# Sums of squares moved ahead of the score maximum, and a Newton step moved off GpSimd, in a six-layer windowed-attention stack

## The chip, the cores and the metric

One core of a Trainium2 chip. The metric is device time of one execution in microseconds (us); each time given for a kernel is the median of several runs. The program uses all engines of the core: TensorE (PE), VectorE (DVE), ScalarE (ACT), GpSimd (POOL) and SyncE (SP) as DMA queue.

## The reference, cut to what matters

The program is four residual blocks on x of shape 2 x 1024 x 128: a 16-head attention with a polynomial in place of softmax, a stack of six layers, a causal softmax attention, and the same stack of six layers again. The stacks are the long part and the only one that changes. One layer of a stack:

```python
def attn_layer(x, Wqkv, qs, ksc, Wo):            # 16 heads of 64, windows of 32
    q, k, v = split(x @ Wqkv)
    q = l2norm(q) * qs
    k = l2norm(k) * ksc
    q = q * cos * scale + rotate_half(q) * sin * scale
    k = k * cos * inv + rotate_half(k) * sin * inv
    return local_attention(q, k, v) @ Wo         # softmax over 64 keys

def ffn_layer(x, g, bln, W1, b1, W2, b2):
    mu = x.mean(-1, keepdims=True)
    var = ((x - mu) ** 2).mean(-1, keepdims=True)
    xn = (x - mu) / jnp.sqrt(var + 1e-05) * g + bln
    a, gate = jnp.split(xn @ W1 + b1, 2, -1)
    return a * gelu(gate) @ W2 + b2

for i in range(6):
    x = attn_layer(shift_tokens(x), ...) + x
    x = ffn_layer(shift_tokens(x), ...) + x
```

All arithmetic here is float32. An inverse root (of a sum of squares of q or k, or of the variance) is taken as a seed y = exp(-0.5 ln v) on ScalarE and one Newton step y(1.5 - 0.5 v y^2).

## The kernel before

`ffn_stack` works in slots. A slot s takes one tile of 128 tokens (16 tiles a layer, 6 layers, 96 tiles a stack, n is the tile's number) through the projections, and in the same slot other stages work on earlier tiles: the scores and the softmax on tile n-1, the transpose of the probabilities on n-2, the product with V on n-3, the output projection on n-4. The feed-forward net works on blocks of four tiles (512 tokens); `feed(s, lag)` gives the block whose turn it is, so that its steps fall into slots by s mod 4, the phase: phase 0 has the centred x, its square and the variance (lag 8) and the last hidden chunk (lag 12); phase 1 has the scaling by the inverse root (lag 9) and the output product (lag 13); phase 2 the three gate products (lag 10); phase 3 the gelu and two hidden chunks (lag 11).

The order on each engine is written out by hand, one function for each engine with a loop over the slots, and semaphores tie them. What each engine does in a slot, in its order:

- TensorE: project q into PSUM banks PQ; transpose the normalised q of n-1 into PT_S (waits `nrm`, 1) and the k (L1233, waits `nrm`, 2); project k into PK; mask and scores of n-1 into PT_S; project v; `values(n-3)`; the first two feed-forward products; then in `feed_third` a wait on `sbd`, by which VectorE says that it has read the scores out of PT_S; in phase 2 the third gate product; `out(s)`, the output projection (L1152, it writes the first bank of PT_S); in phases 0 and 1 a fourth feed-forward product; the transposes of O (L1276, wait `rot` and `sqd` of tile n). Then the next slot's q projection (L1097).
- ScalarE: copy O_T out (L1294); square q into `sq` (L1284, `sqd`); copy q_T, k_T; square k; in phase 3 the gelu; copy V; copy O; exp of the scores (L1332); Ln and Exp of the sums of squares (L1336, L1338, `seeded`); in phase 0 Ln and Exp of the variance (L1342, L1344); in phase 2 three gate copies.
- VectorE: three rope products of q (L1426 to L1429); the transpose of the probabilities (L1460, `ppt`); three rope products of k; row maximum (L1466) and shift (L1469, `sbd`); the two sums of squares (L1435) and their clamp (L1477, `clamped`); row sum (L1480) and its reciprocal (L1484, `rid`); feed-forward steps, among them the variance's epsilon (L1494) in phase 0 and in phase 1 the scaling (L1501) and two H or G writes (L1510); two adds of the output projection (L1515). At the end of a stack also the adds of two SBUF tensors at L1521.
- GpSimd: adds of the rope products of q and k (L1374); a Newton step of four small operations on 128x32 (L1376 to L1382); the products of q and k with the inverse norm (L1386, `nrm`); the product of E with the row's inverse (L1392, `pn`); in phase 0 a Newton step of four operations on 128x512 for the variance (L1396 to L1402, `f_nt`); in phase 1 the bias of xn (L1405).

Of the kernel before, what the change touches and what calls it, by code (L numbers as in the profile page):

```python
# [18 lines left out]
ALU = mybir.AluOpType  # L19
# [835 lines left out]
def ffn_stack(nc, ins, m, call):  # L855
# [6 lines left out]
    with ctx:  # L862
# [3 lines left out]
        def sig(name, per=1):  # L866
# [64 lines left out]
        f_xc, f_sq, f_xcs, f_var, f_eps, f_seed = sig("x_centered"), sig("x_squared"), sig("x_centered_copied"), \  # L931
            sig("var_done"), sig("eps_added"), sig("var_seeded", 2)
        f_nt, f_xn, f_xb = sig("var_newton_steps", 4), sig("xn_scaled"), sig("xn_ready")
        f_g, f_gev, f_ge, f_a, f_hm = sig("gate_done", 3), sig("gate_evacuated", 3), sig("gelu_done"), \
# [34 lines left out]
        def live(s):  # L969

            return 0 <= s < SLOTS
# [10 lines left out]
        def blk(b):  # L982

            return call * (SLOTS // TB) + b
# [295 lines left out]
        def _(act):  # L1280
# [8 lines left out]
            for s in slots:  # L1289
# [30 lines left out]
                if feed(s, 11) is not None:  # L1320
                    nc.scalar.preload_act_table_set("natural_log_exp_and_others")
                if live(s - 3):
                    act.wait_ge(o_mm.sem, o_mm.at(n - 3))
                    act.wait_ge(o_tr.sem, o_tr.past(n - 4))
                    nc.scalar.activation(O[:], PQ, ACT.Copy).then_inc(o_cp.sem, 1)
# [4 lines left out]
                if live(s - 1):  # L1330
                    act.wait_ge(sbd.sem, sbd.at(n - 1))
                    nc.scalar.activation(E[(n - 1) % 2][:], E[(n - 1) % 2][:], ACT.Exp).then_inc(expd.sem, 1)  # L1332
                if live(s):
                    act.wait_ge(clamped.sem, clamped.at(n))
                    act.wait_ge(newton.sem, newton.past(n - 1))
                    nc.scalar.activation(lg[:], ss[n % 2][:], ACT.Ln).then_inc(seeded.sem, 1)  # L1336
                    act.wait_ge(seeded.sem, seeded.at(n, 1))
                    nc.scalar.activation(y0[:], lg[:], ACT.Exp, scale=-0.5).then_inc(seeded.sem, 1)  # L1338
                if (b := feed(s, 8)) is not None:
                    act.wait_ge(f_eps.sem, f_eps.at(blk(b)))  # L1340
                    act.wait_ge(f_nt.sem, f_nt.past(blk(b) - 1))
                    nc.scalar.activation(xsq[:], var[:], ACT.Ln).then_inc(f_seed.sem, 1)  # L1342
                    act.wait_ge(f_seed.sem, f_seed.at(blk(b), 1))
                    nc.scalar.activation(vy0[:], xsq[:], ACT.Exp, scale=-0.5).then_inc(f_seed.sem, 1)  # L1344
                if (b := feed(s, 10)) is not None:
                    act.wait_ge(f_y.sem, f_y.past(blk(b) - 1))
                    for j, (o, k) in enumerate(FCH):
                        act.wait_ge(f_g.sem, f_g.at(blk(b), j + 1))
                        nc.scalar.activation(ge[0:k, j, :], bank((6, 7, 5)[j])[0:k], ACT.Identity,
                                             bias=b1[b // NBLK % 2][0:k, 3 + j:4 + j]).then_inc(f_gev.sem, 1)  # L1350

        @block.gpsimd
        def _(pool):
# [14 lines left out]
            for s in slots:  # L1368
# [20 lines left out]
                if live(s - 1):  # L1389
# [3 lines left out]
                                            ALU.mult).then_inc(pn.sem, 1)  # L1393
                if (b := feed(s, 8)) is not None:
                    pool.wait_ge(f_seed.sem, f_seed.at(blk(b)))
                    nc.gpsimd.tensor_tensor(xsq[:], vy0[:], vy0[:], ALU.mult).then_inc(f_nt.sem, 1)  # L1396
                    pool.wait_ge(f_nt.sem, f_nt.at(blk(b), 1))
                    nc.gpsimd.tensor_tensor(xsq[:], xsq[:], var[:], ALU.mult).then_inc(f_nt.sem, 1)
                    pool.wait_ge(f_nt.sem, f_nt.at(blk(b), 2))
                    nc.gpsimd.tensor_scalar(xsq[:], xsq[:], -0.5, 1.5, ALU.mult, ALU.add).then_inc(f_nt.sem, 1)  # L1400
                    pool.wait_ge(f_nt.sem, f_nt.at(blk(b), 3))
                    nc.gpsimd.tensor_tensor(var[:], xsq[:], vy0[:], ALU.mult).then_inc(f_nt.sem, 1)  # L1402
                if (b := feed(s, 9)) is not None:
# [7 lines left out]
        def _(dve):  # L1411
# [41 lines left out]
            for s in slots:  # L1453
                n = tile(s)
                if live(s):
                    rotate(s, 0, q_mm, PQ)
                if live(s - 2):
                    dve.wait_ge(pn.sem, pn.at(n - 2))
                    dve.wait_ge(pair_in[(n - 3) % 2].sem, pair_in[(n - 3) % 2].past((n - 3) // 2))
                    nc.vector.transpose(PT[:].rearrange("p b t -> p (b t)"), E[n % 2][:]).then_inc(ppt.sem, 1)  # L1460
                if live(s):
                    rotate(s, 1, k_mm, PK)
                if live(s - 1):
                    e = E[(n - 1) % 2]
# [7 lines left out]
                        .then_inc(sbd.sem, 1)  # L1472
                if live(s):
                    sums(n, 0)
                    sums(n, 1)
                    dve.wait_ge(red.sem, red.at(n))
                    nc.vector.tensor_scalar(ss[n % 2][:], ss[n % 2][:], 1e-24, None, ALU.max).then_inc(clamped.sem, 1)  # L1477
                if live(s - 1):
# [16 lines left out]
                if (b := feed(s, 9)) is not None:  # L1495
                    if b % NBLK == 0:
                        dve.wait_ge(ffn_in.sem, ffn_in.at(call * DEPTH + b // NBLK))
                    dve.wait_ge(f_nt.sem, f_nt.at(blk(b)))
                    dve.wait_ge(f_g.sem, f_g.past(blk(b) - 1))
# [97 lines left out]
```

## Time and profile before

| | |
|---|---|
| median of 3 runs | 4362.58 us (4357.62 to 4364.63) |
| the profiled execution | 4365.13 us |
| its span, first to last instruction | 4363.3 us |
| mean granted TensorE clock | 0.974 |
| PE, busy | 3866.2 us, 89% |
| DVE, busy | 3296.5 us, 76% |
| ACT, busy | 2534.1 us, 58% |
| POOL, busy | 2498.8 us, 57% |
| POOL waiting for the seed, L1376 <- L1338 | 476.6 us in 192 times |
| DVE waiting for the square of q, L1426 <- L1284 | 376.2 us in 188 times |

The two stacks lie at about 412 to 2142 us and 2625 to 4356 us of the span; the rest is the two attention blocks. A share of busy time is over the whole span; the shares say which engines have room, not which chain of waits sets a slot's length. For that one follows, within a slot, what each instruction waited for.

### The profile page before, as it was taken

The numbers are of one execution on the slowest core, as the hardware profiler recorded it, in microseconds if no ns is written. First come the engines' busy times: TensorE is split into PE (matmuls) and PEld (weight loads), VectorE is DVE, ScalarE is ACT, GpSimd is POOL, SyncE is SP. The second block draws the span as 40 slices with busy tenths as digits, with TensorE's granted clock in tenths as the row PEclk, the third lists the DMA queues.
The fourth block names the chain that finished last, engine by engine and source line by source line (L and its number), as shares of the span: only waits on it lengthen the run. The fifth ranks groups of instructions, "written<-read, shape, count | busy, mean of one in ns | idle before, by whom it ended". The sixth has DMA issues, their size and how long they took to land. (4 is left out here: it accounts for less than half of the span.)

```text
span 4363.3 us, 151598 instructions
## 1 busy us (share of the span) xinstructions
PE 3866.2 (89%) x66488; PEld 2314.4 (53%) x66488; DVE 3296.5 (76%) x4385; ACT 2534.1 (58%) x3236; POOL 2498.8 (57%) x2036
## 2 busy tenths in 40 slices
PE   6887799999999999999778877899999999999997
PEld 3323456665665666665433334566666666666664
DVE  7997777888888787888454436788888878878884
ACT  6885456566665666666324444556566565666654
POOL 0001677777777777777100005786777777777773
PEclk8999999999999999999789998999999999999998
DMA  0001232332323233222000002323323223232221
GB/s 19 1 1 42 72 87 65 85 77 75 83 67 87 73 78 85 62 67 62 17 1 1 1 14 74 92 62 84 81 67 85 73 79 80 73 81 71 66 60 40
DMA packets 165593, 260.83 MB, mean 60 GB/s; under 512 B 58572, under 2 KB 79816, under 8 KB 164936
## 3 DMA queue, kind: packets, MB, share of 16 engines
q1 hardware_dynamic: 164936, 251.13, 22.2%
q8 instruction: 528, 8.65, 0.9%
q14 instruction: 129, 1.06, 0.1%
HBM read 48.61 MB, written 1.05 MB: 11 GB/s over the span
## 5 line engine op out<-in xcount | busy, mean ns | idle before, releaser
L1374 POOL TENSOR_TENSOR f_k_rotated<-f_rope_ak,f_rope_bk 128x1024 f32<-128x1024 f32 x192 | 454.5, 2367 | 288.7 <-DVE f_rope_bk L1429 288.7
L1097 PE MATMUL banks<-f_wqkv,H 128*128 128x512 f32 x1152 | 564.9, 614 | 17.4 <-DVE f_E L1469 9.2
L1097 PE MATMUL banks<-f_wqkv,G 128*128 128x512 f32 x1152 | 551.8, 601 | 0.0
L1426 DVE TENSOR_TENSOR f_rope_aq<-banks,f_rope 128x1024 f32<-128x1024 f32 x192 | 235.1, 1225 | 389.5 <-ACT f_sqq L1284 376.2
L1361 POOL MEMSET f_kT<- 128x256 f32 x2 | 0.6, 311 | 839.9 <-POOLq L514 460.5
L1374 POOL TENSOR_TENSOR f_q_rotated<-f_rope_aq,f_rope_bq 128x1024 f32<-128x1024 f32 x192 | 454.5, 2367 | 29.0 <-DVE f_rope_bq L1429 28.6
L1319 ACT ACTIVATE f_V<-banks 128x1024 f32<-128x1024 f32 x192 | 196.8, 1025 | 418.7 <-PE banks L1097 418.3
L1152 PEld LDWEIGHTS banks<-f_O_T,f_wo 128*128 128x128 f32 x3072 | 372.6, 192 | 98.3 <-issue 94.6
L1152 PE MATMUL banks<-f_O_T,f_wo 128*128 128x128 f32 x3072 | 375.4, 275 | 6.4 <-issue 5.2
L1392 POOL TENSOR_TENSOR f_E<-f_E,f_row_inverse 128x1024 f32<-128x1024 f32 x192 | 368.6, 1920 | 19.8 <-DVE f_row_inverse L1484 19.8
L1386 POOL TENSOR_TENSOR f_q_rotated<-f_q_rotated,f_inverse_norm 128x1024 f32<-128x1024 f32 x192 | 365.2, 1902 | 15.0
L1386 POOL TENSOR_TENSOR f_k_rotated<-f_k_rotated,f_inverse_norm 128x1024 f32<-128x1024 f32 x192 | 366.2, 1907 | 0.0
L1129 PEld LDWEIGHTS banks<-f_V_previous,f_P_T_paired 64*32 64x32 f32 x12288 | 263.0, 105 | 163.9 <-issue 157.2
L1129 PE MATMUL banks<-f_V,f_P_T_paired 64*32 64x64 f32 x12288 | 323.4, 225 | 17.4 <-issue 16.3
L1426 DVE TENSOR_TENSOR f_rope_ak<-banks,f_rope 128x1024 f32<-128x1024 f32 x192 | 233.4, 1216 | 139.0 <-ACT f_sqk L1284 138.0
L1129 PE MATMUL banks<-f_V_previous,f_P_T_paired 64*32 64x64 f32 x12288 | 316.3, 225 | 12.5 <-issue 8.7
L1233 PE MATMUL banks<-ident,f_k_rotated 128*128 128x128 f32 x1536 | 213.4, 284 | 122.2 <-POOL f_k_rotated L1386 121.9
L1376 POOL TENSOR_TENSOR f_rsqrt_tmp<-f_rsqrt_seed 128x32 f32<-128x32 f32 x192 | 45.9, 239 | 476.6 <-ACT f_rsqrt_seed L1338 476.6
L1114 PEld LDWEIGHTS banks<-f_kT,f_qT 64*32 64x32 f32 x24576 | 271.0, 105 | 86.6 <-issue 62.7
L1114 PE MATMUL banks<-f_kT,f_qT 64*32 64x64 f32 x24576 | 305.1, 225 | 1.6 <-ACT f_kT L1307 1.5
L1138 PE MATMUL banks<-f_xn,f_w 128*128 128x512 f32 (+1 forms) x576 | 287.6, 623 | 19.1 <-DVE H L1510 12.0
L1460 DVE STREAM_TRANSPOSE f_P_T<-f_E 128x1024 f32<-128x1024 f32 x192 | 238.1, 1240 | 86.9 <-POOL f_E L1392 86.7
(207 smaller groups left out, 8961.6 us busy)
## 6 DMA issues: line engine op xcount, KB each, us to landing
f_P_T_paired<-f_P_T SPq DMA_DIRECT2D x1536, 64.0 KB
f_V_previous<-f_V SPq DMA_DIRECT2D x192, 384.0 KB, 3.7
f_V_previous<-f_V SPq DMA_DIRECT2D x192, 128.0 KB, 2.4
f_wqkv<-in_L_ffn_Wqkv SPq DMA_DIRECT2D x48, 384.0 KB, 4.1
f_rope<-in_rope SPq DMA_DIRECT2D x24, 512.0 KB, 5.1
f_wo<-in_L_ffn_Wo SPq DMA_DIRECT2D x12, 512.0 KB, 5.4
f_w<-in_L_ffn_W SPq DMA_DIRECT2D x12, 341.0 KB
f_w<-in_L_ffn_W SPq DMA_DIRECT2D x24, 64.0 KB
```

Source lines behind the costliest of these rows:

```text
L1097: mm = nc.tensor.matmul(ps[:, o * BLK:(o + 1) * BLK], xs, w[:, c * INNER + o * BLK:c * INNER + (o + 1) * BLK], start=True, stop=True)
L1114: mm = nc.tensor.matmul(PT_S[g * W:(g + 1) * W, c:c + 2 * W], qT[rows, k, g * W:(g + 1) * W], kT[u][rows, k, g * W:(g + 2) * W], start=Fal ...
L1129: mm = nc.tensor.matmul(PQ[g * W:(g + 1) * W, a * BLK + j * DH:a * BLK + (j + 1) * DH], F[n % 2][r, t, c * W:(c + 1) * W], of[n % len(of)] ...
L1138: nc.tensor.matmul(banks[0:k, bk * BLK:(bk + 1) * BLK], w1[b // NBLK % 2][:, half * DI + o:half * DI + o + k], xn[:], start=True, stop=Tru ...
L1152: mm = nc.tensor.matmul(bank(4, P), wo[layer(s - 4) % 2][:, k, :], OT[n % 2][:, :, m2, hh * 2 * W:(hh + 1) * 2 * W], start=k == 0, stop=k ...
L1233: mm = nc.tensor.transpose(PV_F[:, k * P:(k + 1) * P], qk[1][:, k * P:(k + 1) * P], ident[:])
L1319: nc.scalar.activation(V[n % 4][:], PV_F, ACT.Copy).then_inc(v_ev.sem, 1)
L1374: nc.gpsimd.tensor_tensor(qk[i][:], ra[i][:], rb[i][:], ALU.add).then_inc(radd.sem, 1)
L1386: nc.gpsimd.tensor_tensor(heads_of(qk[i][:]), heads_of(qk[i][:]), over(rn[:, i * HEADS:(i + 1) * HEADS], DH), ALU.mult)\
L1392: nc.gpsimd.tensor_tensor(e, e, ri[:].unsqueeze(1).unsqueeze(3).to_broadcast([P, 2, HEADS, W]), ALU.mult).then_inc(pn.sem, 1)
L1426: nc.vector.tensor_tensor(heads_of(ra[i][:]), src, table(2 * i, 0, DH), ALU.mult).then_inc(rot.sem, 1)
L1460: nc.vector.transpose(PT[:].rearrange("p b t -> p (b t)"), E[n % 2][:]).then_inc(ppt.sem, 1)
```

## The change

Three edits, all in `ffn_stack`.

1. VectorE's order: `sums(n, 0)` now stands right behind the rope products of q (ahead of L1460), and `sums(n, 1)` with the clamp right behind the rope products of k, ahead of the row maximum and the shift.
2. ScalarE's order: Ln and Exp of the sums of squares now stand behind the copy of V, ahead of the copy of O, the square of the centred x and the exp of the scores.
3. The variance's Newton step: GpSimd's four operations go. ScalarE squares the seed behind its Exp, in phase 0; VectorE does the rest in two operations in phase 1, ahead of the scaling.

```diff
@@ scalar
+                if live(s):
+                    act.wait_ge(clamped.sem, clamped.at(n))
+                    act.wait_ge(newton.sem, newton.past(n - 1))
+                    nc.scalar.activation(lg[:], ss[n % 2][:], ACT.Ln).then_inc(seeded.sem, 1)
+                    act.wait_ge(seeded.sem, seeded.at(n, 1))
+                    nc.scalar.activation(y0[:], lg[:], ACT.Exp, scale=-0.5).then_inc(seeded.sem, 1)
                 if live(s - 3):
                     act.wait_ge(o_mm.sem, o_mm.at(n - 3))
...
-                if live(s):
...
-                    nc.scalar.activation(y0[:], lg[:], ACT.Exp, scale=-0.5).then_inc(seeded.sem, 1)
...
                     nc.scalar.activation(vy0[:], xsq[:], ACT.Exp, scale=-0.5).then_inc(f_seed.sem, 1)
+                    act.wait_ge(f_seed.sem, f_seed.at(blk(b), 2))
+                    nc.scalar.activation(xsq[:], vy0[:], ACT.Square).then_inc(f_seed.sem, 1)
@@ gpsimd
-                if (b := feed(s, 8)) is not None:
-                    pool.wait_ge(f_seed.sem, f_seed.at(blk(b)))
-                    nc.gpsimd.tensor_tensor(xsq[:], vy0[:], vy0[:], ALU.mult).then_inc(f_nt.sem, 1)
...
-                    nc.gpsimd.tensor_tensor(var[:], xsq[:], vy0[:], ALU.mult).then_inc(f_nt.sem, 1)
@@ vector
                 if live(s):
                     rotate(s, 0, q_mm, PQ)
+                    sums(n, 0)
                 if live(s - 2):
...
                 if live(s):
                     rotate(s, 1, k_mm, PK)
+                    sums(n, 1)
+                    dve.wait_ge(red.sem, red.at(n))
+                    nc.vector.tensor_scalar(ss[n % 2][:], ss[n % 2][:], 1e-24, None, ALU.max).then_inc(clamped.sem, 1)
                 if live(s - 1):
...
-                if live(s):
-                    sums(n, 0)
-                    sums(n, 1)
...
                 if (b := feed(s, 9)) is not None:
...
+                    dve.wait_ge(f_seed.sem, f_seed.at(blk(b)))
+                    nc.vector.scalar_tensor_tensor(xsq[:], var[:], -0.5, xsq[:], ALU.mult, ALU.mult).then_inc(f_nt.sem, 1)
+                    dve.wait_ge(f_nt.sem, f_nt.at(blk(b), 1))
+                    nc.vector.scalar_tensor_tensor(var[:], xsq[:], 1.5, vy0[:], ALU.add, ALU.mult).then_inc(f_nt.sem, 1)
```

The sizes of the semaphores `f_seed` (2 to 3 steps) and `f_nt` (4 to 2) follow.

VectorE in the middle of a slot, before:

```order
L1426 TENSOR_TENSOR f_rope_aq<-banks,f_rope 128x1024
L1427 TENSOR_TENSOR f_rope_bq<-banks,f_rope 128x16x32
L1429 TENSOR_TENSOR f_rope_bq<-banks,f_rope 128x16x32
L1460 STREAM_TRANSPOSE f_P_T<-f_E 128x1024
L1426 TENSOR_TENSOR f_rope_ak<-banks,f_rope 128x1024
L1427 TENSOR_TENSOR f_rope_bk<-banks,f_rope 128x16x32
L1429 TENSOR_TENSOR f_rope_bk<-banks,f_rope 128x16x32
L1466 TENSOR_REDUCE f_row_max<-banks 128x16
L1469 TENSOR_TENSOR f_E<-banks,f_row_max 128x16x2x32
L1435 TENSOR_REDUCE f_sum_of_squares<-f_sqq 128x16
L1435 TENSOR_REDUCE f_sum_of_squares<-f_sqk 128x16
L1477 TENSOR_SCALAR f_sum_of_squares<-f_sum_of_squares 128x32
```

and now:

```order
L1419 TENSOR_TENSOR f_rope_aq<-banks,f_rope 128x1024
L1420 TENSOR_TENSOR f_rope_bq<-banks,f_rope 128x16x32
L1422 TENSOR_TENSOR f_rope_bq<-banks,f_rope 128x16x32
L1428 TENSOR_REDUCE f_sum_of_squares<-f_sqq 128x16
L1454 STREAM_TRANSPOSE f_P_T<-f_E 128x1024
L1419 TENSOR_TENSOR f_rope_ak<-banks,f_rope 128x1024
L1420 TENSOR_TENSOR f_rope_bk<-banks,f_rope 128x16x32
L1422 TENSOR_TENSOR f_rope_bk<-banks,f_rope 128x16x32
L1428 TENSOR_REDUCE f_sum_of_squares<-f_sqk 128x16
L1459 TENSOR_SCALAR f_sum_of_squares<-f_sum_of_squares 128x32
L1463 TENSOR_REDUCE f_row_max<-banks 128x16
L1466 TENSOR_TENSOR f_E<-banks,f_row_max 128x16x2x32
```

Both sums and the clamp have moved ahead of the row maximum and the shift (L1469 before, L1466 now).

VectorE at the end of a slot of phase 1, now:

```order
L1472 TENSOR_REDUCE f_row_sum<-f_E 128x16
L1476 RECIPROCAL f_row_inverse<-f_row_sum 128x16
L1491 SCALAR_TENSOR_TENSOR f_x_squared<-f_var_then_rstd,f_x_squared 128x512
L1493 SCALAR_TENSOR_TENSOR f_var_then_rstd<-f_x_squared,f_var_seed 128x512
L1497 SCALAR_TENSOR_TENSOR f_xn<-f_x_centered,f_ln_g_ln_b_b_1,f_var_then_rstd 128x512
L1506 SCALAR_TENSOR_TENSOR H<-banks,f_ln_g_ln_b_b_1,G 64x512 x2
L1511 TENSOR_TENSOR G<-banks,G 64x128 x2
```

The rows L1491 and L1493 are new there; both read two tensors in SBUF.

ScalarE at the end of a slot of phase 0, now:

```order
L1325 ACTIVATE f_log_sum<-f_sum_of_squares 128x32
L1327 ACTIVATE f_rsqrt_seed<-f_log_sum 128x32
L1331 ACTIVATE f_O<-banks 128x1024
L1335 ACTIVATE f_x_squared<-banks 128x512
L1338 ACTIVATE f_E<-f_E 128x1024
L1342 ACTIVATE f_x_squared<-f_var_then_rstd 128x512
L1344 ACTIVATE f_var_seed<-f_x_squared 128x512
L1346 ACTIVATE f_x_squared<-f_var_seed 128x512
L1294 ACTIVATE f_O_T<-banks 128x1024
L1284 ACTIVATE f_sqq<-banks 128x1024
```

L1346 is new, ahead of the O_T copy and the next slot's square of q; the two 128x32 rows stood behind the exp of f_E before.

## Rows read from the trace of the kernel before

**Rows 1.** Busy time by engine over most of the first stack: window, its length, each engine's busy us (instructions), granted PE clock, DMA share, GB/s.
```profile
620.00:2060.00 1440.00, 1353.54 (x26343) 873.93 (x26343) 1171.07 (x1505) 883.06 (x1107) 1078.56 (x876) 1.00 0.29 74
```

**Rows 2.** Who waited for whom, TensorE: total us, times, longest.
```profile
PE banks L1233 <- POOL f_k_rotated L1386: 121.9, 182, 1.2
```

**Rows 3.** Timeline of GpSimd, phase 2 and the next: start us, us, engine, line, operation.
```profile
1008.54 2.36 POOL L1374 TENSOR_TENSOR f_k_rotated<-f_rope_ak,f_rope_bk 128x1024 f32<-128x1024 f32 x1 [1.73 <-DVE f_rope_bk L1429]
...
1014.58 0.22 POOL L1380 TENSOR_SCALAR f_rsqrt_tmp<-f_rsqrt_tmp 128x32 f32<-128x32 f32 x1
...
1015.21 1.90 POOL L1386 TENSOR_TENSOR f_q_rotated<-f_q_rotated,f_inverse_norm 128x1024 f32<-128x1024 f32 x1
1017.07 1.90 POOL L1386 TENSOR_TENSOR f_k_rotated<-f_k_rotated,f_inverse_norm 128x1024 f32<-128x1024 f32 x1
...
1031.63 0.22 POOL L1380 TENSOR_SCALAR f_rsqrt_tmp<-f_rsqrt_tmp 128x32 f32<-128x32 f32 x1
```

**Rows 4.** Timeline of VectorE, one slot of phase 1.
```profile
1053.91 1.22 DVE L1426 TENSOR_TENSOR f_rope_aq<-banks,f_rope 128x1024 f32<-128x1024 f32 x1 [2.77 <-ACT f_sqq L1284]
...
1056.25 1.23 DVE L1460 STREAM_TRANSPOSE f_P_T<-f_E 128x1024 f32<-128x1024 f32 x1
1057.41 1.19 DVE L1426 TENSOR_TENSOR f_rope_ak<-banks,f_rope 128x1024 f32<-128x1024 f32 x1
...
1059.71 1.21 DVE L1466 TENSOR_REDUCE f_row_max<-banks 128x16 f32<-128x1024 f32 x1
1060.95 1.23 DVE L1469 TENSOR_TENSOR f_E<-banks,f_row_max 128x1024 f32<-128x1024 f32 x1
1062.09 1.21 DVE L1435 TENSOR_REDUCE f_sum_of_squares<-f_sqq 128x16 f32<-128x1024 f32 x1
1063.22 1.21 DVE L1435 TENSOR_REDUCE f_sum_of_squares<-f_sqk 128x16 f32<-128x1024 f32 x1
...
1064.56 1.21 DVE L1480 TENSOR_REDUCE f_row_sum<-f_E 128x16 f32<-128x1024 f32 x1
...
1065.97 0.69 DVE L1501 SCALAR_TENSOR_TENSOR f_xn<-f_x_centered,f_ln_g_ln_b_b,f_var_then_rstd 128x512 f32<-128x512 f32 x1
...
1068.32 0.61 DVE L1515 TENSOR_TENSOR H<-banks,H 64x128 f32<-64x128 f32 x2
```

**Rows 5.** Timeline of VectorE, a later slot of phase 1, 14 blocks on.
```profile
2032.16 0.69 DVE L1501 SCALAR_TENSOR_TENSOR f_xn<-f_x_centered,f_ln_g_ln_b_b,f_var_then_rstd 128x512 f32<-128x512 f32 x1
```

**Rows 6.** Timeline of TensorE, end of a slot of phase 2 and start of the next.
```profile
1013.42 1.95 PE L1152 MATMUL banks<-f_O_T,f_wo 128*128 128x128 f32 x16
1015.21 1.04 PE L1276 MATMUL banks<-ident,f_O 128*128 128x128 f32 x8
1016.08 1.88 PE L1097 MATMUL banks<-f_wqkv,H 128*128 128x512 f32 x4
```

**Rows 7.** Timeline of ScalarE, end of a slot of phase 0 and start of the next.
```profile
1050.66 0.63 ACT L1342 ACTIVATE f_x_squared<-f_var_then_rstd 128x512 f32<-128x512 f32 x1 [2.71 <-DVE f_var_then_rstd L1494]
...
1051.86 1.01 ACT L1294 ACTIVATE f_O_T<-banks 128x1024 f32<-128x1024 f32 x1
1052.76 1.02 ACT L1284 ACTIVATE f_sqq<-banks 128x1024 f32<-128x1024 f32 x1
```

**Rows 8.** Timeline of VectorE: the shift in that slot of phase 0.
```profile
1043.73 1.22 DVE L1469 TENSOR_TENSOR f_E<-banks,f_row_max 128x1024 f32<-128x1024 f32 x1
```

**Rows 9.** Timeline of VectorE: the adds at L1521 beside GpSimd's products, and alone.
```profile
2050.50 4.35 DVE L1521 TENSOR_TENSOR X<-X,H 64x512 f32<-64x512 f32 x2
...
2102.60 1.40 DVE L1521 TENSOR_TENSOR X<-X,H 64x512 f32<-64x512 f32 x2
```

**Rows 10.** Timeline of GpSimd: the k product that runs beside those adds.
```profile
2051.95 2.35 POOL L1386 TENSOR_TENSOR f_k_rotated<-f_k_rotated,f_inverse_norm 128x1024 f32<-128x1024 f32 x1
```

**Rows 11.** Timeline of TensorE: transposes after a long wait near the first stack's start.
```profile
464.94 1.97 PE L1227 MATMUL banks<-ident,f_q_rotated 128*128 128x128 f32 x8 [4.25 <-POOL f_q_rotated L1386]
```

**Rows 12.** Busy time and granted clock in the stretch that begins there, columns as in rows 1.
```profile
465.00:470.00 5.00, 5.00 (x18) 3.95 (x19) 1.34 (x2) 2.21 (x3) 5.00 (x3) 0.50 0.00 2
```

More of the change, by code:

```diff
@@ L931, in ffn_stack @@
         f_xc, f_sq, f_xcs, f_var, f_eps, f_seed = sig("x_centered"), sig("x_squared"), sig("x_centered_copied"), \
-            sig("var_done"), sig("eps_added"), sig("var_seeded", 2)
-        f_nt, f_xn, f_xb = sig("var_newton_steps", 4), sig("xn_scaled"), sig("xn_ready")
+            sig("var_done"), sig("eps_added"), sig("var_seeded", 3)
+        f_nt, f_xn, f_xb = sig("var_newton_steps", 2), sig("xn_scaled"), sig("xn_ready")
         f_g, f_gev, f_ge, f_a, f_hm = sig("gate_done", 3), sig("gate_evacuated", 3), sig("gelu_done"), \
@@ L1332, in _ @@
                     nc.scalar.activation(E[(n - 1) % 2][:], E[(n - 1) % 2][:], ACT.Exp).then_inc(expd.sem, 1)
-                if live(s):
[L1334 to L1337, printed above, removed]
-                    nc.scalar.activation(y0[:], lg[:], ACT.Exp, scale=-0.5).then_inc(seeded.sem, 1)
                 if (b := feed(s, 8)) is not None:
@@ L1393, in _ @@
                                             ALU.mult).then_inc(pn.sem, 1)
-                if (b := feed(s, 8)) is not None:
-                    pool.wait_ge(f_seed.sem, f_seed.at(blk(b)))
-                    nc.gpsimd.tensor_tensor(xsq[:], vy0[:], vy0[:], ALU.mult).then_inc(f_nt.sem, 1)
[L1397 to L1401, printed above, removed]
-                    nc.gpsimd.tensor_tensor(var[:], xsq[:], vy0[:], ALU.mult).then_inc(f_nt.sem, 1)
                 if (b := feed(s, 9)) is not None:
@@ L1472, in _ @@
                         .then_inc(sbd.sem, 1)
-                if live(s):
-                    sums(n, 0)
-                    sums(n, 1)
-                    dve.wait_ge(red.sem, red.at(n))
-                    nc.vector.tensor_scalar(ss[n % 2][:], ss[n % 2][:], 1e-24, None, ALU.max).then_inc(clamped.sem, 1)
                 if live(s - 1):
```

## The prediction

> **What bounds the kernel now.** I read the busy times first. Over most of the first stack TensorE is busy 1353.54 of 1440 us at full clock [rows 1], and no other engine comes near; a slot there lasts 17.25 us, so TensorE's own work is 17.25 x 0.94 = 16.2 and about 1 us a slot is waiting. The 17.25 comes from the scaling in phase 1, which recurs every four slots: (2032.16 - 1065.97) / 14 = 69.0 us a group [rows 4, 5]. The list of waits says whom TensorE waits for: the normalised k, 121.9 us in 182 times [rows 2]. GpSimd's timeline shows a period free of jitter, 1014.58 to 1031.63, 17.05 us [rows 3]. So I followed the chain of k backwards: k transposed and the next k projected on TensorE, squared, rope products, row maximum, shift, both sums and clamp on VectorE, Ln and Exp, then on GpSimd the Newton step and the products of q and k, and transposed again. That is a loop over one slot, and its sum is the 17.05. The change cuts this loop. The question is what the next loop is.
>
> **The change, part by part.** *The k loop.* The clamp of k now comes before the row maximum and the shift (59.71 to 62.09, 2.38 us) and without the sum of q behind them (1.13) [rows 4]: 3.5 us earlier. GpSimd must first finish its add of k, 2.36 us [rows 3], so 3.0 of it arrives and the loop falls to 14.05. It no longer binds.
>
> *The loop through the shift.* TensorE may not write the output projection before VectorE has read the scores (`sbd`). Write S for the end of the shift. From S the loop runs: output projection 1.79, transposes of O 0.87, q projection 1.88 [rows 6], square 1.02 [rows 7], hand-overs 0.3 together, then VectorE from the rope of q to the next S. Before, VectorE's part was 53.91 to 62.18, 8.27 us back to back [rows 4], so the loop was 14.1 in phase 3 and hidden. Now both sums and the clamp lie in it: 1.13 + 1.34 (63.22 to 64.56, clamp included) = 2.47 [rows 4], together **10.74**. The distance from S to the rope of q, by phase:
> - phase 3: 5.85, the sum above.
> - phase 2: a third gate product of 512 columns ahead, half a projection [rows 6], 0.9: 6.75.
> - phase 0: here ScalarE is late. Before, Ln of the variance began at 1050.66 [rows 7], 5.7 behind the shift (1043.73 + 1.22) [rows 8]. VectorE now reaches the row sum 1.2 behind S (it waits for the exp) where it was 2.4 (62.18 to 64.56) [rows 4], so Ln begins at 4.5. Ln to square 2.10 [rows 7], the new Square 0.66 priced as the Ln beside it, square and hand-over 1.15: 8.4.
> - phase 1, if nothing is in the way: row sum at 1.2, 1.41 to the Newton operations, two of 0.74 (the scaling's 0.69 and a semaphore), scaling to G 2.35, G 0.55 [rows 4]: 7.0.
>
> *The Newton operations on VectorE are in the way of GpSimd.* Each reads two tensors in SBUF. The trace has one such operation of 512 elements beside GpSimd's large products: the two adds at L1521 take 4.35 us there and 1.40 alone [rows 9]. They end 0.55 behind the k product, and that product itself takes 2.35 in place of 1.90 [rows 3, 10]. So the two engines take turns, each waiting for the other's whole instruction. The Trainium skill (SBUF — State Buffer, Who interferes with whom) says the same as a rule: a VectorE instruction with two SBUF inputs and a GpSimd instruction that reads SBUF share a port, and the later one waits for the earlier to finish; the trace agrees. It speaks against putting these two operations here. Where do they fall? The rope of k ends 3.75 ahead of S; GpSimd's add of k ends at S - 1.3, Newton takes 1.3, the q product runs from 0 to 1.85, the k product to 3.75, the E product from there [rows 3]. The first operation, ready at 2.6, waits to 3.75 and ends at 4.3. The E product, held up, ends at 6.05. The second waits for it and ends at 6.6. Scaling from 6.65, G at 9.0, the rope at **9.55** instead of 7.0.
>
> *GpSimd* loses four operations a block, none of them on the new loop: worth nothing between the ends of a stack. *ScalarE's* earlier Ln and Exp (0.5 us) delay the copy of O; it is still done 0.8 ahead of S, while O's transposes start 1.9 behind S. Nothing.
>
> *TensorE's clock.* The slot from a phase-1 S to the next is 9.55 + 10.74 = 20.3 long; TensorE works 16.2 of it and has only the one place to wait: 4.1 us in one piece. After a wait of 4.25 the eight transposes took 1.97 us [rows 11], against 1.04 for the same shape [rows 6], and the granted clock was 0.50, the 1.2 GHz level, for the next 5 us [rows 12]. Here the third gate product, output projection, transposes and q projection follow, 5.4 us, all in the loop. Bounds: nothing, or half of 5 us, 2.5. I take 1.0, as the wait is a little shorter than the row's and TensorE comes from full use. The Trainium skill (TensorE: Matmul & The Clock Gate) likewise has an idle array fall back to 1.2 GHz.
>
> *Sum.* A group of four slots: 6.75 + 5.85 + 8.4 + 9.55 + 4 x 10.74 = 73.5, with the clock 74.5, against 69.0: +5.5. There are 44 full groups in the two stacks: +242. At the start of a stack there is no feed-forward yet and for four slots no output projection, so the new loop beats the 17.05 by 1 to 3 us in six slots: I estimate -11 a stack (0 to -15). Behind the last tile of a stack the k product is over at S + 3.75, some 4 earlier for TensorE, and two variances pass without GpSimd's Newton, which I put at 2 each: an estimate of -9 a stack (0 to -12). Together -40. Net +202 on the profiled execution's 4365.13, that is 4567; the median stands 2.5 below it: **4565**.
>
> **The rivals.**
> - *The port costs nothing.* The operations slip between GpSimd's, or the adds at L1521 were slow for a reason of their own. Group 70.95, +1.95, total +86 - 40: 4409. Against it: both sides are held up at once [rows 9, 10]; for it: few places in the trace show it.
> - *TensorE becomes the bound: faster.* If the shift came before TensorE reaches the output projection, the only limit were its 16.2 [rows 1]: 1.05 x 176 slots = -185: 4180. This decides once the loop through the shift is under 16.2 on average; I have 17.7 even without the port. It would take 1.5 us a slot of overlap that I have not seen, though VectorE runs back to back in [rows 4]. Here the Trainium skill (Perfetto Trace Analysis, Identifying the Most-Contended Engine) would have one look: the most occupied engine is what to work on. That is TensorE in this trace, yet it is a chain that holds it up.
> - *No change.* The port is free and my loop is 1 us a group too long: 4363, within 0.2%.
> - *The clock falls fully in each group*, +2.5: 4565 + 66 = 4631.
>
> That the edits don't reach the program is excluded: the order of instructions shows each.
>
> **How the numbers follow.** Forecast (shift loop, port blocked, some clock) 0.68; port free 0.14; clock fully lost 0.09; TensorE-bound 0.06; no change 0.03. A measurement of this kernel tells about 0.2%, 9 us, from no change. Faster 0.06, same 0.03, slower 0.91. The range goes from the free port to just above the lost clock, 4405 to 4640, which leaves out the faster case and the tails. The likeliest case alone, blocked with a clock loss from 0 to 1.5: 4521 to 4587.
>
> **What would show it.** TensorE's waits for the normalised q and k all but vanish, and in their place stand waits for the shift (f_E, L1466 now) ahead of L1152, some 1.5 to 2 us a slot and 4 in phase 2. VectorE runs from the rope of q to the shift in 10.7. In phase 1 the operations at L1491 and L1493 together take about 4 us where two of 0.7 would do, and the E product 2.35. Groups of 73 to 75 us. GpSimd's busy time falls. I am wrong if TensorE still meets the shift done, if L1491 and L1493 take 1.4 together, or if the rope of q follows S by much more than the sums above, above all in phase 0, where ScalarE's Square stands ahead of the O_T copy.

## The result, and the profile after

The changed kernel takes 4841.75 us (median of 4 runs, 4826.33 to 4842.86) against 4363.60 (4357.62 to 4365.05): a ratio of 1.109, 95% interval 1.1066 to 1.1115. It is 478 us slower. The forecast was 4565, slower by 202, and its range ended at 4640: the direction was right, the size was missed by more than half.

| | before | after |
|---|---|---|
| span | 4363.3 us | 4839.3 us |
| mean granted TensorE clock | 0.974 | 0.937 |
| PE, busy | 3866.2 us, 89% | 4020.0 us, 83% |
| DVE, busy | 3296.5 us, 76% | 3671.2 us, 76% |
| ACT, busy | 2534.1 us, 58% | 2537.3 us, 52% |
| POOL, busy | 2498.8 us, 57% | 2306.3 us, 48% |

First the stretch of [rows 1] in the kernel after, columns as there:
```profile
620.00:2060.00 1440.00, 1228.68 (x22702) 794.73 (x22700) 1150.33 (x1331) 762.46 (x970) 857.54 (x686) 0.95 0.26 66
```
TensorE does 14% fewer matmuls in the same 1440 us, and its granted clock is 0.95 where it was 1.00. Then TensorE's waits of the kernel after, beside [rows 2]:
```profile
PE banks L1152 <- DVE f_E L1466: 332.3, 132, 4.4
PE banks L1227 <- DVE G L1511: 48.9, 22, 3.6
...
PE banks L1138 <- DVE f_E L1466: 45.7, 44, 1.7
PE banks L1227 <- DVE H L1511: 45.0, 22, 3.6
...
PE banks L1233 <- POOL f_k_rotated L1388: 0.8, 1, 0.8
```
The wait for the normalised k is gone (121.9 us to 0.8), as forecast; 332 us of waits for the shift ahead of the output projection (L1152) stand in its place, and 46 more ahead of the third gate product of phase 2 (L1138). The two lines at L1227 were not forecast: 44 times, once a group, the transposes of q wait for the addition to G or H.

VectorE of the kernel after, the end of one slot of phase 0 and then the slot of phase 1, to be read against [rows 4]:
```profile
1070.12 1.31 DVE L1459 TENSOR_SCALAR f_sum_of_squares<-f_sum_of_squares 128x32 f32<-128x32 f32 x1
1071.34 1.21 DVE L1463 TENSOR_REDUCE f_row_max<-banks 128x16 f32<-128x1024 f32 x1
1072.59 1.23 DVE L1466 TENSOR_TENSOR f_E<-banks,f_row_max 128x1024 f32<-128x1024 f32 x1
1074.94 1.22 DVE L1472 TENSOR_REDUCE f_row_sum<-f_E 128x16 f32<-128x1024 f32 x1 [1.12 <-ACT f_E L1338]
1076.19 0.25 DVE L1476 RECIPROCAL f_row_inverse<-f_row_sum 128x16 f32<-128x16 f32 x1
1076.36 1.26 DVE L1491 SCALAR_TENSOR_TENSOR f_x_squared<-f_var_then_rstd,f_x_squared 128x512 f32<-128x512 f32 x1
1077.65 2.28 DVE L1493 SCALAR_TENSOR_TENSOR f_var_then_rstd<-f_x_squared,f_var_seed 128x512 f32<-128x512 f32 x1
1079.97 0.75 DVE L1497 SCALAR_TENSOR_TENSOR f_xn<-f_x_centered,f_ln_g_ln_b_b,f_var_then_rstd 128x512 f32<-128x512 f32 x1
...
1082.20 0.61 DVE L1511 TENSOR_TENSOR G<-banks,G 64x128 f32<-64x128 f32 x2
1082.84 1.22 DVE L1419 TENSOR_TENSOR f_rope_aq<-banks,f_rope 128x1024 f32<-128x1024 f32 x1
```
GpSimd of the same kernel over the same time, beside [rows 3]:
```profile
1069.04 2.35 POOL L1376 TENSOR_TENSOR f_k_rotated<-f_rope_ak,f_rope_bk 128x1024 f32<-128x1024 f32 x1 [2.22 <-DVE f_rope_bk L1422]
...
1075.17 1.90 POOL L1388 TENSOR_TENSOR f_k_rotated<-f_k_rotated,f_inverse_norm 128x1024 f32<-128x1024 f32 x1
1077.03 2.36 POOL L1394 TENSOR_TENSOR f_E<-f_E,f_row_inverse 128x1024 f32<-128x1024 f32 x1
```
Read the ends. The clamp (L1459) starts at 1070.12 and took 0.18 us before, so it should end at 1070.30; it ends at 1071.43, with GpSimd's add of k (1071.39). The first Newton operation ends behind the k product (1077.62 and 1077.07), the E product behind that (1079.39), the second Newton operation last (1079.93). That second part is the forecast's; the clamp is not. TensorE after that slot:
```profile
1077.49 1.88 PE L1097 MATMUL banks<-f_wqkv,H 128*128 128x512 f32 x4
1082.96 1.94 PE L1227 MATMUL banks<-ident,f_q_rotated 128*128 128x128 f32 x8 [3.59 <-DVE G L1511]
```
It waits 3.59 us for G (1082.81) and then takes 1.94 us for eight transposes, about the 1.97 of [rows 11]; the granted clock from 1082.9 to 1085 is 0.50, the 1.2 GHz level.

The two distances of the shift loop, in us, means over slots 8 to 95 of both stacks, from VectorE's timeline; a line's "rope to S" is the stretch that follows its "S to rope", so it lies in the next slot:

| phase | S to rope: before | forecast | after | rope to S: before | forecast | after |
|---|---|---|---|---|---|---|
| 0 | 9.05 | 8.4 | 8.87 | 8.29 | 10.74 | 11.86 |
| 1 | 7.58 | 9.55 | 9.08 | 9.81 | 10.74 | 12.69 |
| 2 | 8.19 | 6.75 | 6.72 | 8.90 | 10.74 | 11.86 |
| 3 | 6.98 | 5.85 | 6.74 | 10.14 | 10.74 | 11.86 |

A group takes 79.7 us, forecast 74.5, before 68.9. From the first rope of a stack to the shift of its eighth tile (the head, below) it takes 158.5 and 156.5 us (before 145.1 and 146.4), where 11 less was forecast.

### The profile page after: what moved, and what is told of

It reads as the page before. It is cut to its first block and busy times, and to the rows that moved or that the text cites. A ratio compares the mean times of both kernels' runs of the same rounds, so it can differ in the third digit from the quotient of the medians.

```text
span 4839.3 us, 151550 instructions
## 1 busy us (share of the span) xinstructions
PE 4020.0 (83%) x66488; PEld 2428.5 (50%) x66488; DVE 3671.2 (76%) x4481; ACT 2537.3 (52%) x3284; POOL 2306.3 (48%) x1844
## 5 line engine op out<-in xcount | busy, mean ns | idle before, releaser
L1152 PE MATMUL banks<-f_O_T,f_wo 128*128 128x128 f32 x3072 | 488.8, 325 | 367.5 <-DVE f_E L1466 332.3
L1152 PEld LDWEIGHTS banks<-f_O_T,f_wo 128*128 128x128 f32 x3072 | 453.5, 232 | 504.7 <-DVE f_E L1466 432.4
L1294 ACT ACTIVATE f_O_T<-banks 128x1024 f32<-128x1024 f32 x192 | 195.8, 1020 | 393.7 <-PE banks L1276 393.7
L1472 DVE TENSOR_REDUCE f_row_sum<-f_E 128x16 f32<-128x1024 f32 x192 | 234.2, 1220 | 219.3 <-ACT f_E L1338 219.3
L1394 POOL TENSOR_TENSOR f_E<-f_E,f_row_inverse 128x1024 f32<-128x1024 f32 x192 | 386.9, 2015 | 23.0 <-DVE f_row_inverse L1476 23.0
L1138 PE MATMUL banks<-f_xn,f_w 128*128 128x512 f32 (+1 forms) x576 | 295.8, 624 | 59.5 <-DVE f_E L1466 45.7
L1114 PEld LDWEIGHTS banks<-f_kT,f_qT 64*32 64x32 f32 x24576 | 255.6, 105 | 100.8 <-issue 61.9
L1097 PEld LDWEIGHTS banks<-f_wqkv,H 128*128 128x128 f32 x1152 | 204.8, 198 | 194.7 <-issue 183.7
L1114 PE MATMUL banks<-f_kT,f_qT 64*32 64x64 f32 x24576 | 287.5, 225 | 15.6 <-ACT f_kT L1307 15.0
L815 DVE TENSOR_REDUCE soft_neg_max<-banks 128x3 f32<-128x1536 f32 (+11 forms) x219 | 176.6, 853 | 159.6 <-PE banks L706 107.2
```

The source lines that it names most:

```text
L1097: mm = nc.tensor.matmul(ps[:, o * BLK:(o + 1) * BLK], xs, w[:, c * INNER + o * BLK:c * INNER + (o + 1) * BLK], start=True, stop=True)
L1114: mm = nc.tensor.matmul(PT_S[g * W:(g + 1) * W, c:c + 2 * W], qT[rows, k, g * W:(g + 1) * W], kT[u][rows, k, g * W:(g + 2) * W], start=Fal ...
L1138: nc.tensor.matmul(banks[0:k, bk * BLK:(bk + 1) * BLK], w1[b // NBLK % 2][:, half * DI + o:half * DI + o + k], xn[:], start=True, stop=Tru ...
L1152: mm = nc.tensor.matmul(bank(4, P), wo[layer(s - 4) % 2][:, k, :], OT[n % 2][:, :, m2, hh * 2 * W:(hh + 1) * 2 * W], start=k == 0, stop=k ...
L1294: nc.scalar.activation(OT[n % 2][:].rearrange("p a k t -> p (a k t)"), PK, ACT.Copy)\
L1394: nc.gpsimd.tensor_tensor(e, e, ri[:].unsqueeze(1).unsqueeze(3).to_broadcast([P, 2, HEADS, W]), ALU.mult).then_inc(pn.sem, 1)
```

## The experiments

The kernel before, run again beside them, had medians of 4360.9 to 4364.5 us.

**The two parts of the change apart.** The changed kernel with the four Newton operations of the variance on GpSimd again (they come back as they were; what goes from ScalarE and VectorE is):
```diff
-                    nc.scalar.activation(xsq[:], vy0[:], ACT.Square).then_inc(f_seed.sem, 1)
...
-                    nc.vector.scalar_tensor_tensor(xsq[:], var[:], -0.5, xsq[:], ALU.mult, ALU.mult).then_inc(f_nt.sem, 1)
-                    dve.wait_ge(f_nt.sem, f_nt.at(blk(b), 1))
-                    nc.vector.scalar_tensor_tensor(var[:], xsq[:], 1.5, vy0[:], ALU.add, ALU.mult).then_inc(f_nt.sem, 1)
```


> The change without its third part: sums, clamp and Ln/Exp moved as in the change, the variance's Newton step back on GpSimd. Theory (the loop through the shift, lengthened by the sums and by a clamp that waits for GpSimd's add, sets the slot; Newton on VectorE adds its own share in phase 1): rope of q to shift end stays 11.86 us in all phases, the clamp 1.31; the phase-1 distance from shift to the rope of q falls from 9.1 to about 7.6, the phase-0 one by 0.6; group 76.7 against 79.7, total about 4720 us. Rival (the two Newton operations on VectorE are the main loss, as the prediction's largest single term had it): group near 70, total about 4410.

Measured: 4806.87 us (4800.25 to 4817.27), ratio 1.1016 [1.0997, 1.1035]. And the kernel before with only that edit made:

> The kernel before with only the third part of the change: Newton of the variance on ScalarE and VectorE. Theory (two-SBUF-input operations of VectorE and GpSimd's products take turns): L-lines of the two new operations above 0.7 us each, the rope of q of the next slot late by some 3 us once in four slots, group 71.5 to 72, total about 4495 us. Rival (the k loop of 17.05 hides all of it, and GpSimd is relieved): 4355 to 4370 us.

Measured: 4473.67 us (4469.58 to 4480.66), ratio 1.0252 [1.0237, 1.0267], a group of 71.6. The new order alone costs 442 us, 87 more than I expected by then, and the Newton step alone 109; together they cost 478. The clamp took 1.31 us and rope to S 11.86, as expected; the 87 lie in S to rope, which is 8.18, 8.34, 7.69 and 7.12 us in phases 0 to 3. ScalarE's new order of Ln and Exp is part of both this kernel and the change and was not run apart.

**The clamp as another instruction.** In the changed kernel, the clamp takes the maximum over a pair (sum, 1e-24) with a reduction:
```diff
+        sp2 = sb("sum_and_floor", [P, 2 * HEADS, 2])
...
+            nc.gpsimd.memset(sp2[:], 1e-24).then_inc(cleared.sem, 1)
...
-                nc.vector.tensor_reduce(ss[n % 2][:, i * HEADS:(i + 1) * HEADS], heads_of(sq[i][:]), AX.X, ALU.add)\
+                nc.vector.tensor_reduce(sp2[:, i * HEADS:(i + 1) * HEADS, 0], heads_of(sq[i][:]), AX.X, ALU.add)\
...
-                    nc.vector.tensor_scalar(ss[n % 2][:], ss[n % 2][:], 1e-24, None, ALU.max).then_inc(clamped.sem, 1)
+                    nc.vector.tensor_reduce(ss[n % 2][:], sp2[:], AX.X, ALU.max).then_inc(clamped.sem, 1)
```


> The change with the clamp in another form at the same place: the sums are written beside a constant 1e-24 and a tensor_reduce max over the pair takes the place of the tensor_scalar max; same values. Theory (the tensor_scalar of SBUF to SBUF needs what GpSimd's add of k holds): the reduce takes about 0.2 us, rope to shift end 10.75, group 75 (with some of the clock's loss gone), total about 4610 us. Rival (the clamp is slow because it waits for the reduce right in front of it): 1.3 us again, 4840 us.

Measured: 4644.9 us (4641.74 to 4648.07), ratio 1.0643 [1.0627, 1.0658]: 197 us back, where about 230 were expected. Its VectorE, and under it its GpSimd:
```profile
520.19 1.20 DVE L1430 TENSOR_REDUCE f_sum_and_floor<-f_sqk 128x16 f32<-128x1024 f32 x1
521.42 0.22 DVE L1461 TENSOR_REDUCE f_sum_of_squares<-f_sum_and_floor 128x32 f32<-128x64 f32 x1
521.56 1.22 DVE L1465 TENSOR_REDUCE f_row_max<-banks 128x16 f32<-128x1024 f32 x1
```
```profile
520.35 2.34 POOL L1378 TENSOR_TENSOR f_k_rotated<-f_rope_ak,f_rope_bk 128x1024 f32<-128x1024 f32 x1 [2.21 <-DVE f_rope_bk L1424]
```
The reduction starts 1.07 us into GpSimd's add and takes 0.22 us; the tensor_scalar in that place took 1.31. All 192 of each do so (1.30 to 1.33 us, and 0.22), in the groups by line of the changed kernel and of this one:
```profile
L1459 DVE TENSOR_SCALAR f_sum_of_squares<-f_sum_of_squares 128x32 f32<-128x32 f32 x192 | 251.9, 1312 | 6.6
```
```profile
L1461 DVE TENSOR_REDUCE f_sum_of_squares<-f_sum_and_floor 128x32 f32<-128x64 f32 x192 | 42.2, 220 | 6.6
```
The values and the semaphore that it waits for are the same; the kind of instruction differs, and the reduction even reads twice as many elements, from a tile of its own. Rope to S falls to 10.77, the forecast's 10.74, in three phases (12.90 in phase 1), and S to rope is 8.34, 9.37, 6.75 and 5.89: the forecast's four distances to within 0.2. The 12.90 is 2.1 over: TensorE's waits for the addition to G or H are 169 us in 46 times here. The Trainium skill (SBUF — State Buffer, Who interferes with whom) has this as a rule: tensor_scalar can take both ports and then contends with GpSimd, tensor_reduce never does. By that rule the clamp's place was as exposed as the Newton operations'; the trace agrees, with 1.31 against 0.22.

**TensorE kept busy ahead of its wait.** In the changed kernel, filler matmuls into a bank that is free at the time (m is 3 in a stack's first eight slots, else 1, and none in phase 2):
```diff
+                if live(s - 3) and live(s) and (m := 3 if s < 8 else (0 if s % TB == 2 else 1)):
...
+                        nc.tensor.matmul(PK[:, o * BLK:(o + 1) * BLK], state(s)[:, col(s):col(s) + P],
+                                         wqkv[layer(s) % 2][:, o * BLK:(o + 1) * BLK], start=True, stop=True)
                 if live(s - 1):
                     pe.wait_ge(sbd.sem, sbd.at(tile(s) - 1))
```


> The change with idle-time matmuls: before TensorE waits for the shift it runs extra 128x512 products into PK, whose readers are done, nobody reads them; three in the first eight slots of a stack, one in phases 0, 1 and 3, none in phase 2. Theory (the wait for the shift lets the granted clock fall to 1.2 GHz, and the output projection behind it is in the loop): L1152 in the first slots 2.0 us in place of 3.76, shift to rope of q 5.9 in phase 3 in place of 6.74; group down by 1 to 1.5, total 4760 to 4790 us. Rival (the clock's fall is beside the loop): 4840 us, or a little more for the extra work.

Measured: 4790.23 us (4782.11 to 4796.02), ratio 1.0975 [1.0956, 1.0995]: adding work gives 51 us back, at the edge of what was expected. In phase 3 the rope of q is 5.89 us behind S again, for 6.74. The same filler, one in phase 2 too, in the kernel with the sums alone:

> The changed kernel with the Newton step of the feed-forward variance back on GpSimd (4807 when run, group 78.8), with filler matmuls on TensorE ahead of its wait for the shift: three in a stack's first eight slots, one in every later slot. With the tensor_scalar floor each group is 8.0 us longer than with the tensor_reduce floor (70.8): 4.4 of it are the floor's own (4 x 1.09, rope of q to shift 11.86 for 10.77), and 3.6 stand from shift to rope of q. If those 3.6 are TensorE's clock: from shift to rope 7.7, 6.8, 6.75 and 5.9, a group of 74.5 to 75, 4580 to 4620. Rival, they are port or queue waits elsewhere: no more than 50 us faster, 4760 or more.

Measured: 4630.51 us (4621.97 to 4635.0), ratio 1.0616 [1.06, 1.0631]: 176 us back, 10 short of the range, with 7.38 us from S to rope in phase 1 where 6.8 was expected. TensorE in the head of the first stack without filler, and with:
```profile
515.26 3.75 PE L1152 MATMUL banks<-f_O_T,f_wo 128*128 128x128 f32 x16 [4.40 <-issue]
518.80 1.49 PE L1276 MATMUL banks<-ident,f_O 128*128 128x128 f32 x8
```
```profile
508.30 2.84 PE L1192 MATMUL banks<-f_wqkv,H 128*128 128x512 f32 x6
512.55 2.05 PE L1152 MATMUL banks<-f_O_T,f_wo 128*128 128x128 f32 x16 [1.41 <-DVE f_E L1480]
514.44 1.04 PE L1283 MATMUL banks<-ident,f_O 128*128 128x128 f32 x8
```
Behind a wait of 4.40 us the output projection takes 3.75 us; with the filler (L1192) the wait is 1.41 and it takes 2.05. The granted clock is 0.50 from 515 to 519 us in the first and 1.00 from 512 to 516 in the second. The transposes, the q projection and so the next rope wait for it. The rival of that run (waits elsewhere) falls.

**The order alone, without the clamp's wait.** The Newton step on GpSimd and the clamp as reduction, then with filler (as in the 4790 run):

> The changed kernel with two parts taken back: the floor of the sums is a tensor_reduce (a maximum of the pair sum, 1e-24) instead of the tensor_scalar, and the Newton step of the feed-forward variance is on GpSimd again. What is left is the new order alone: both sums ahead of the shift. If the port wait of the floor, the port waits of the Newton step and TensorE's clock are all that went over the forecast, then from rope of q to shift 10.8 us in all four phases, and from shift to rope of q 8.4, 7.0 to 8.3, 6.75 and 5.9: a group of 71 to 72.5 us, 4440 to 4510 us in all (4364 + 44 x 2.1 to 3.6, with head and tail at -10). Rival, the sums on the chain that ends in the shift cost more than their 2.5 us: over 4560.

> As the run before it, with one matmul of filler on TensorE (three in a stack's first eight slots, none in phase 2) where it stands idle ahead of the shift, so that its clock stays up. If what is left over the arithmetic is the clock alone: 8.3 + 7.0 + 6.75 + 5.9 from shift to rope and 4 x 10.77, a group of 71.1 us, 4430 to 4460. Rival, the clock is not part of it: no change against the run before, or some us slower for the filler.

Measured: 4438.61 us (4435.89 to 4441.92), ratio 1.0178 [1.0163, 1.0193], and 4401.86 (4398.43 to 4404.05), ratio 1.0092 [1.0075, 1.0109]. The groups are 70.8 and 70.2; 4438.61 lies 1.4 below its range and 4402 lies 28 below the other, as the rope of q is 7.7 us behind S in phase 0, and 6.75 in phase 1, where I had 8.3 and 7.0, and the two heads are 8 and 10 us shorter than before. So the new order is still slower than the old one when nothing is in its way: the shift loop is longer than the k loop it replaces. On top of 4402, what filler gives back adds 37, the Newton step on ScalarE and VectorE another 206 (4438.61 to 4644.9), and the clamp's wait 197 (to 4841.75). The 206 are 4.8 us a group: 2.0 in phase 1 from S to rope (9.37 for 7.36), 2.1 behind it, where TensorE waits for G (12.90 for 10.78), and 0.65 in phase 0, where ScalarE squares the seed (8.34 for 7.69).

The parts do not add. The clamp's wait costs 197 us with the Newton step on VectorE, 368 without (4806.87 to 4438.61), and 229 where filler keeps the clock up (4630.51 to 4401.86); its own 1.09 us in 192 slots are 209. Of the 159 by which 368 is over 209, filler takes 139 back; the last 20 are not explained. Why the kernel with both parts loses less of it (S to rope 6.72 in phase 2, against 7.69 with the sums alone) stays open.

**Where on VectorE the Newton step does its harm.** In the 4474 run its two operations take 0.63 and 0.69, not blocked at all, where I had expected more than 0.7 each, and yet it is 109 us slower. Its VectorE and then its TensorE:
```profile
1013.09 0.69 DVE L1494 SCALAR_TENSOR_TENSOR f_var_then_rstd<-f_x_squared,f_var_seed 128x512 f32<-128x512 f32 x1
...
1016.05 0.61 DVE L1512 TENSOR_TENSOR G<-banks,G 64x128 f32<-64x128 f32 x2
```
```profile
1016.80 1.06 PE L1227 MATMUL banks<-ident,f_q_rotated 128*128 128x128 f32 x8 [1.69 <-DVE G L1512]
1018.34 1.86 PE L1233 MATMUL banks<-ident,f_k_rotated 128*128 128x128 f32 x8 [0.47 <-POOL f_k_rotated L1388]
1019.99 2.81 PE L1097 MATMUL banks<-f_wqkv,H 128*128 128x512 f32 x4
```
G is done 8.0 us behind the shift, 1.4 later than before (means of 7.95 and 6.55). TensorE waits for it, and then goes at half clock for the transposes of k (1.86 us for 1.04) and most of the k projection (2.81 for 1.88), on which the rope of k waits. That is 1.7 of the 2.7 us by which a group is longer (11.52 us from rope to S behind phase 1, for 9.81). Another 0.4 is VectorE's own, as it comes to the rope of q behind G, and 0.6 lies in phase 0 (S to rope 9.67 for 9.05), where ScalarE squares the seed ahead of the square of q; that square was not tried apart. So I moved the Newton operations and the scaling behind the additions to H and G (the block of `feed(s, 9)`, unchanged, to behind that of `live(s - 4)`):

> The kernel before with the Newton step on ScalarE and VectorE (4474 when run, group 71.6), and with the Newton step and the scaling of xn behind the additions to H and G on VectorE in the same slot. In the 4474 run the two new operations take only 0.63 and 0.69 us, but push the addition to G back by 1.4 us, TensorE's transposes of q wait 1.7 us for it, and the rest of its work runs at half clock. If that is the cost: group 69.0 to 69.6, 4365 to 4395. Rival, the cost is GpSimd's, whose products beside VectorE's two-SBUF-operand operations take 4.22 us a pair instead of 3.77 and whose Newton operations 0.76 and 0.68 instead of 0.22 and 0.57: it stays at 4450 to 4475.

Measured: 4495.4 us (4492.18 to 4501.31), ratio 1.0309 [1.0294, 1.0325]. No gain, 22 us worse, and my theory had left something out. The wait for G is gone from TensorE's list, but now all three operations meet GpSimd's products. VectorE, and GpSimd under it:
```profile
1016.71 0.90 DVE L1506 SCALAR_TENSOR_TENSOR f_x_squared<-f_var_then_rstd,f_x_squared 128x512 f32<-128x512 f32 x1
1017.64 2.27 DVE L1508 SCALAR_TENSOR_TENSOR f_var_then_rstd<-f_x_squared,f_var_seed 128x512 f32<-128x512 f32 x1
1019.95 2.28 DVE L1512 SCALAR_TENSOR_TENSOR f_xn<-f_x_centered,f_ln_g_ln_b_b,f_var_then_rstd 128x512 f32<-128x512 f32 x1
```
```profile
1017.02 2.35 POOL L1388 TENSOR_TENSOR f_k_rotated<-f_k_rotated,f_inverse_norm 128x1024 f32<-128x1024 f32 x1
1019.33 2.35 POOL L1394 TENSOR_TENSOR f_E<-f_E,f_row_inverse 128x1024 f32<-128x1024 f32 x1
```
They take 5.5 us instead of 2.1, and the rope of q is late. Ahead of H and G they hold up TensorE, behind them they are held up themselves: neither of the two places was cheap.

**Half of the order: a kernel faster than both.** The sum of q alone goes ahead; the sum of k and the clamp stay behind the shift, where GpSimd's add of k is over. On the kernel before:
```diff
                     rotate(s, 0, q_mm, PQ)
+                    sums(n, 0)
...
                 if live(s):
-                    sums(n, 0)
                     sums(n, 1)
```


> The kernel before with one edit: the sum of squares of q goes behind the rope of q (ahead of the transpose of E), the sum of k, the floor and everything else stay behind the shift. Theory: the kernel before is bound by the loop through k's norms, 17.05 us a slot, of which this takes 1.13; the loop through the shift gets 1.13 more: 8.27 + 1.13 = 9.40 from rope of q to shift, and 8.4 + 7.0 + 6.75 + 5.85 from shift to rope, 65.6 us a group as a floor (63.7 by the k loop), 65.6 to 66.8 with the clock: 4210 to 4280 us. Rival, the loop through the shift is what bounds the kernel before, or the late rope of k costs its 0.6 us a slot and the k loop gives nothing back: 4364 to 4470.

Measured: 4300.24 us (4291.01 to 4307.15), ratio 0.9859 [0.9844, 0.9874]: 61 us (1.4%) faster than before and 542 faster than the change, if 20 short of the range. Its VectorE, and under it its GpSimd and TensorE:
```profile
994.55 1.21 DVE L1435 TENSOR_REDUCE f_sum_of_squares<-f_sqk 128x16 f32<-128x1024 f32 x1
995.79 0.18 DVE L1477 TENSOR_SCALAR f_sum_of_squares<-f_sum_of_squares 128x32 f32<-128x32 f32 x1
...
1005.00 1.21 DVE L1435 TENSOR_REDUCE f_sum_of_squares<-f_sqq 128x16 f32<-128x1024 f32 x1
```
```profile
992.32 2.36 POOL L1374 TENSOR_TENSOR f_k_rotated<-f_rope_ak,f_rope_bk 128x1024 f32<-128x1024 f32 x1 [1.73 <-DVE f_rope_bk L1429]
```
```profile
994.25 2.84 PE L1138 MATMUL banks<-f_xn,f_w 128*128 128x512 f32 x6
996.93 1.95 PE L1152 MATMUL banks<-f_O_T,f_wo 128*128 128x128 f32 x16
```
GpSimd's add of k ends at 994.68, and the same tensor_scalar, at 995.79, takes 0.18 us (0.20 in the mean of 192). A group is 67.7 for the 65.6 worked out: from S in phase 3 to the next S it is 15.96, which fits the k loop (the 17.05 of [rows 3] less 1.13), and in phase 2 S to rope is 7.87 for 6.75. There TensorE no longer waits for the shift: S is at 994.64, and TensorE, at full clock (granted 1.00), has only just begun the three gate products (2.84 us), so the output projection starts 2.3 us behind S. It is busy for 19.9 of the 21 us from 978 to 999; in this phase TensorE's own work, and not the shift, sets the distance. The last try put Ln and Exp of the norms ahead of the Exp of E on ScalarE as well, with the clamp as reduction:

> The kernel of the run with the sum of q alone ahead (4300, group 67.7), with the floor as tensor_reduce and with Ln and Exp of the norms ahead of the Exp of E on ScalarE, behind the copy of O. In the 4300 run Ln starts 0.25 us after the floor is done. If the k loop bounds it: 0.2 us a slot where it does, 4265 to 4290. Rival, the Exp of E ends 1.1 us later, with it the row sum and the addition to G on VectorE, for which TensorE's transposes wait in phase 1: 4300 to 4350.

Measured: 4450.19 us (4449.08 to 4454.06), ratio 1.0207 [1.019, 1.0224]. The rival was right in kind and too small. TensorE:
```profile
1004.64 1.88 PE L1228 MATMUL banks<-ident,f_q_rotated 128*128 128x128 f32 x8 [2.39 <-DVE G L1517]
```
The row sum starts 2.88 us behind S for 1.25, the scaling then takes 1.36 for 0.71, and G is done at 7.74 for 5.39 (means in phase 1). The same wait of TensorE is back, with a granted clock of 0.53 behind it: 150 us, where the rival had at most 50. A group is 3.4 us longer: 1.5 behind the wait for G, 1.1 ahead of it, as VectorE comes to the rope of q behind G, and 0.7 in phase 0, where Ln of the variance starts 0.7 later.

## Why the prediction was right or wrong

**What held.** The loop through k is off the path; the loop through the shift is the one that binds, and both sums lie in it. With the clamp's wait taken away the loop has the forecast's lengths in seven of its eight places (10.77 for 10.74; 5.89, 6.75, 8.34 and 9.37 for 5.85, 6.75, 8.4 and 9.55); the eighth is 12.90 for 10.74. The Newton operations and GpSimd take turns as said: 1.26 and 2.28 us with the E product at 2.36 between them.

**The step that failed** is the 10.74. It priced the clamp inside the 1.34 of [rows 4], where it runs 0.18 us with GpSimd between two operations. The same text says of GpSimd that its add of k ends at S - 1.3, and the clamp now stands just ahead of the row maximum and the shift (it ends 2.5 us before S): the two numbers together put the clamp into the add. I had the rule for the Newton operations and applied it to instructions with two SBUF inputs only. It cost 4 x 1.09 = 4.4 us of the 5.2 by which a group exceeded the forecast, 0.1 more lies in the hand-overs, and 0.8 in phase 1's rope to S, 12.69 for 11.86. Without the clamp's wait the kernel takes 4644.9 us: 197 of the 277 by which the forecast fell short.

**That 0.8** is a wait I had not looked for: I moved G late (9.0 behind S) and followed VectorE on to the rope of q, but not TensorE, whose transposes of q wait for the addition to G; the square of k and the rope of k follow from them. It takes 0.8 us a group here and 2.1 where the clamp does not wait (12.90 for 10.77). The forecast gave TensorE only the one place to wait. The 4474, 4495 and 4450 runs show this wait on, off and on again.

**The clock** was put at 1.0 a group from 0 to 2.5, and only in phase 2. From S to rope the sum of all phases came out at 31.4 where 31.55 with that 1.0 was forecast: right in sum and wrong in place. The waits for the shift come in all phases, 0.9 is lost in phase 3 and 0.5 in phase 0 (with filler, in the 4790 run, both are gone: 5.89 and 8.37), none in phase 2, and phase 1 is 0.5 shorter than its arithmetic. Where it was badly off is the **head**, forecast at -11 a stack: there TensorE has the most idle time, and behind waits of 3.9 to 4.4 us the whole output projection runs at half clock (3.75 us). Slots that take 16.66 us in the 4402 kernel took 19.3 to 20.4; 1.1 of the difference is the clamp's wait, the rest went with filler (17.75 in the 4790 run). Measured +13 and +10. With filler the head of the 4402 kernel is 137 and 136 us, 8 and 10 under the kernel before, the estimate's size.

Over the whole span: the body +462 us for +242, the heads +24 for -22, the rest with the tails -10 for -18; together +476, the difference of the spans. The 4645 kernel has +285, +1 and -9: without the clamp's wait the body is 43 over the forecast, which is the wait for G less 1.2 us a group from S to rope, and the heads 23. Of the rivals, the lost clock was a real one but was priced at phase 2 alone; neither the faster case nor the free port is left.

## What to carry to other kernels

Before a short operation is moved, write down what the other engine runs at its new time and which kind of instruction it is: 0.18 us may be 1.31 a slot there, and a reduction in its place 0.22. When an operation ends later, follow every engine that waits for it, not only its own. Move as little of a loop's work as takes it off the path: one of the two sums ahead beat both kernels.

## What the runs showed of the hardware

- A tensor_scalar of 128x32, from SBUF to SBUF, that is ready in the middle of GpSimd's tensor_tensor of 128x1024 ends with it: 1312 ns in the mean of 192, 187 ns without. The rope products (PSUM and SBUF in) and the reductions beside the same operations kept their times.
- GpSimd pays as well. Its small operations for the norms, 0.22 and 0.25 us (0.22 and 0.57 in phase 1 of the kernel before, beside VectorE's scaling), take 0.76 and 0.68 beside VectorE's Newton operations in the 4474 run, and a product of 1.90 takes 2.36.
- Extra matmuls on TensorE, whose results nothing reads, made a kernel 176 us faster (4806.87 to 4630.51), as the work that follows the wait is the path and runs at 2.4 instead of 1.2 GHz (granted clock 1.00 for 0.50 in the stretches shown).
